# A scan kernel's strip products regrouped: bursts of two slots round the four strips, one bank for the exponents

## What is computed

```python
z, xBC, dt_raw = split(u @ in_proj_w.T)          # z 1024, x 1024, B 128, C 128, dt 64 columns
xBC = silu(conv4(xBC) + conv_b)                  # causal, 4 taps
dt = softplus(dt_raw + dt_bias);  dA = -exp(A_log) * dt
# chunks of 64 tokens, 64 heads of 16 columns; cs = cumsum(dA) in the chunk
Y_diag = sum_s (C_c . B_s) * exp(cs_c - cs_s) * dt_s * x_s     # s <= c, within the chunk
states = sum_s B_s * exp(cs_end - cs_s) * dt_s * x_s           # carried from chunk to chunk
Y_off  = (C_c . state before) * exp(cs_c)
y = Y_diag + Y_off + x * D
yg = y * silu(z);  out = (yg * rsqrt(mean(yg^2) + eps) * norm_w) @ out_proj_w.T
```

## Time and profile before

| | |
|---|---|
| runs | 2022.22, 2024.91, 2026.64 us; median 2024.91 |
| profiled execution | 2034.44 us, its span 2032.5 us |
| busy in the span | PE 1847.0 us (91%), DVE 1419.1 (70%), POOL 983.9 (48%), ACT 921.0 (45%) |
| mean granted TensorE clock | 0.969 of full speed |

### The profile page before, as it was taken

One profiled execution on the slowest core, in us unless ns is written; L12 is line 12 of the kernel. 1 busy time (PEld: TensorE's weight loads), 2 busy tenths in 40 slices (PEclk: granted clock), 3 DMA queues, 4 the chain that ended last, 5 costly groups with the idle time before them and its releaser, 6 DMA issues. The chain is left out here.

```text
span 2032.5 us, 37312 instructions
## 1 busy us (share of the span) xinstructions
PE 1847.0 (91%) x11168; PEld 986.0 (49%) x11168; DVE 1419.1 (70%) x2295; ACT 921.0 (45%) x1647; POOL 983.9 (48%) x1031
## 2 busy tenths in 40 slices
PE   3699999989998998998999899898999999999998
PEld 1255555646545555554654555655334334334333
DVE  6758668666857766875875676875776766765765
ACT  2453354253444334425334434423664654754753
POOL 0045345434525434542542543555764764764754
PEclk9899999999999999999989999889999999999999
DMA  6110140131122014113012201813010110110110
GB/s 200 46 45 25 40 104 26 34 75 39 43 48 80 24 45 101 25 39 86 28 42 55 68 24 50 212 34 71 7 57 32 34 59 26 36 62 26 36 42 31
DMA packets 212566, 109.54 MB, mean 54 GB/s; under 512 B 131642, under 2 KB 183542, under 8 KB 212390
## 3 DMA queue, kind: packets, MB, share of 16 engines
q1 hardware_dynamic: 212390, 107.37, 19.8%
HBM read 80.57 MB, written 26.76 MB: 53 GB/s over the span
## 5 line engine op out<-in xcount | busy, mean ns | idle before, releaser
L1015 ACT ACTIVATE decay<-ps_d 128x512 f32<-128x512 f32 x256 | 151.7, 593 | 383.1 <-PE ps_d L766 381.8
L777 PE MATMUL ps_yd<-mix,xpad 128*32 128x64 f32 x4096 | 281.6, 226 | 31.7 <-DVE y L1326 30.7
L777 PEld LDWEIGHTS ps_yd<-mix,xpad 128*32 128x32 f32 x4096 | 242.6, 113 | 122.6 <-issue 93.2
L1600 POOL TENSOR_TENSOR xend<-xpad,decay 128x256 f32<-128x256 f32 x256 | 180.6, 725 | 228.3 <-PE ps_yo L799 198.2
L708 PE MATMUL ps_in<-u_hi,w_hi 128*128 128x512 f16 (+1 forms) x608 | 238.5, 392 | 52.8 <-DVE u_lo L1188 32.3
L1290 DVE TENSOR_TENSOR mix<-decay,gb 128x512 f32<-128x512 f32 x256 | 222.4, 874 | 54.9 <-ACT gb L1002 31.9
L708 PE MATMUL ps_in<-u_lo,w_hi 128*128 128x512 f16 (+1 forms) x608 | 237.7, 391 | 0.0
L708 PE MATMUL ps_in<-u_hi,w_lo 128*128 128x512 f16 (+1 forms) x608 | 236.9, 390 | 0.0
L730 PE MATMUL ps_in<-w_out,zg 128*128 128x512 f32 x512 | 230.8, 604 | 6.7 <-DVE pre L1201 6.7
L1201 DVE SCALAR_TENSOR_TENSOR pre<-ps_in,cws,pre 128x511 f32<-128x511 f32 (+2 forms) x240 | 178.8, 745 | 14.2 <-ACT pre L954 8.4
L954 ACT ACTIVATE pre<-ps_in,cb,cws 128x512 f32<-128x512 f32 x80 | 62.2, 777 | 231.9 <-PE ps_in L708 231.9
(11 more groups left out here) (194 smaller groups left out, 3877.2 us busy)
## 6 DMA issues: line engine op xcount, KB each, us to landing
ebc<-e_dram SPq DMA_DIRECT2D x256, 64.0 KB, 2.6
u<-u_t SPq DMA_DIRECT2D x9, 1024.0 KB, 5.1
res<-u_tok SPq DMA_DIRECT2D x32, 256.0 KB, 2.7
x_dram<-res SPq DMA_DIRECT2D x32, 256.0 KB, 2.0
xa<-x_dram SPq DMA_DIRECT2D x8, 1024.0 KB, 6.1
xr<-x_dram SPq DMA_DIRECT2D x32, 256.0 KB, 2.7
out<-xr SPq DMA_DIRECT2D x32, 256.0 KB, 2.0
fw_words<-gu_words SPq DMA_DIRECT2D x32, 176.0 KB, 2.7
```

The source lines that it names most:

```text
L777: last = mm(ps_yd[g * 32:(g + 1) * 32, k * CH:(k + 1) * CH], xpad[:, c % 2, k * NG + g, :], mix[:, g, k, :], start=True, stop=True, tile_p ...
L1015: ac(decay[:, n % NG, :, :].rearrange("p a b -> p (a b)"), ps_d[n % 2][:, :], ACT.Exp).then_inc(e_done, 1)
L1600: g_.tensor_tensor(xend[:, g:NP:NG, :], xpad[:, c % 2, g:NP:NG, :], decay[:, g, :, CH - 1:CH].broadcast_to([P, CT, 2 * HD]), ALU.mult).the ...
```

## The change

- **Strips.** The groups of heads are cut anew: group g now holds 8 neighbouring pairs of heads (g x 8 to g x 8 + 7) instead of every fourth. The 8 products of a group then go to the strips 0, 1, 2, 3, 0, 1, 2, 3 (`strip = e % NG`) instead of all to strip g.
- **Bursts.** TensorE does `within` of two slots together, at the second of them (g = 1 and g = 3), after the slot's projection.
- **Banks.** ps_yd becomes two banks, one for even and one for odd chunks; ps_d becomes one. The strip products of chunk c wait for y_all of chunk c - 2, and the exponent product of slot n for the exponential of slot n - 1. The feed-forward phase takes the same eight banks in another order.
- **Order.** y_all goes from VectorE's slot g = 0 to g = 1, behind mixing; gate from g = 1 to 2, square from 2 to 3, sum_squares from g = 3 to g = 0 of the chunk after; q0, q1, q2 to slots 13, 21, 29.
- **DMAs.** ld_dram and the constant rows are laid out by the new groups: 18 stores of the parts for a batch instead of 6, 17 loads of constants instead of 9. load_head is called at SyncE's slot 28 instead of 30.

The diff, cut to its core:

```diff
-BODY_USES = [..., (11, "x0"), (12, "q0"), (14, "o0"), ..., (20, "q1"), (22, "o1"), ..., (28, "q2"), (30, "o2")]
+BODY_USES = [..., (11, "x0"), (13, "q0"), (14, "o0"), ..., (21, "q1"), (22, "o1"), ..., (29, "q2"), (30, "o2")]
-        ps_d = [bank("ps_d0"), bank("ps_d1")]
-        ps_t, ps_s, ps_yd, ps_yo = bank("ps_t"), bank("ps_s"), bank("ps_yd"), bank("ps_yo")
+        ps_d = bank("ps_d")
+        ps_yd = [bank("ps_yd0"), bank("ps_yd1")]
+        ps_t, ps_s, ps_yo = bank("ps_t"), bank("ps_s"), bank("ps_yo")
...
-        ps_gu = [ps_yd] + ps_d + ps_in + [ps_t, ps_s, ps_yo]
+        ps_gu = [ps_yd[1], ps_d, ps_yd[0]] + ps_in + [ps_t, ps_s, ps_yo]
...
                     for h2 in range(2):
-                        sp.dma_start(ld_dram[b, :, :, h2, t].rearrange("r q t -> q r t"),
-                                     ld_parts[row + h2 * NP:row + (h2 + 1) * NP, :, :]).then_inc(parts_out, 16)
+                        for j in range(NG):
+                            heads = slice(row + h2 * NP + j * CT, row + h2 * NP + (j + 1) * CT)
+                            sp.dma_start(ld_dram[b, :, :, j, h2, t].rearrange("r e t -> e r t"), ld_parts[heads, :, :])\
+                              .then_inc(parts_out, 16)
...
-                    if n == 30 and st.proj is not None:
+                    if n == 28 and st.proj is not None:
                         load_head(b + 1)
...
             def exponents(b, n):
-                need(pe, e_done, b * SLOTS + n - 1)
-                mm(ps_d[n % 2][:, :].rearrange("p (k t) -> p k t", k=CT), lhs_d[0:94, c % 2, g, :],
-                   rhs_d[0:94, c % 2, g:NP:NG, :], start=True, stop=True).then_inc(d_full, 1)
+                need(pe, e_done, b * SLOTS + n)
+                mm(ps_d[:, :].rearrange("p (k t) -> p k t", k=CT), lhs_d[0:94, c % 2, g, :],
+                   rhs_d[0:94, c % 2, g * CT:(g + 1) * CT, :], start=True, stop=True).then_inc(d_full, 1)
...
             def within(b, n):
                 if g == 0:
                     pe.wait_ge(t_free, (b * NC + c) * NA + 3)
-                    need(pe, y_done, b * NC + c)
-                for k in range(CT):
-                    last = mm(ps_yd[g * 32:(g + 1) * 32, k * CH:(k + 1) * CH], xpad[:, c % 2, k * NG + g, :],
-                              mix[:, g, k, :], start=True, stop=True, tile_position=(0, g * 32))
+                    need(pe, y_done, b * NC + c - 1)
+                for e in range(CT):
+                    tile, strip = 2 * g + e // NG, e % NG
+                    last = mm(ps_yd[c % 2][strip * 32:(strip + 1) * 32, tile * CH:(tile + 1) * CH],
+                              xpad[:, c % 2, g * CT + e, :], mix[:, g, e, :], start=True, stop=True,
+                              tile_position=(0, strip * 32))
...
                     use_in(st, n)
-                    within(b, n)
+                    if g % 2 == 1:
+                        within(b, n - 1)
+                        within(b, n)
                     if g == 1 and c > 0:
                         from_before(b, c)
...
-                    if g == 0 and c > 0:          # VectorE
-                        y_all(b, c - 1)
                     if n + 2 < SLOTS:
                         mixing(b, n + 2)
                     if g == 0 and c > 0:
                         add_state(b, c - 1, 0)
                         add_state(b, c - 1, 1)
+                    if g == 1 and c > 0:
+                        y_all(b, c - 1)
...
-                    if g == 1 and c > 0:          # GpSimd
+                    if g == 2 and c > 0:
                         gate(st, c - 1)
...
-                    if g == 3 and c > 0:
-                        sum_squares(b, c - 1)
+                    if g == 0 and c > 1:
+                        sum_squares(b, c - 2)
...
+                sum_squares(b, NC - 2)
                 gate(st, NC - 1)
                 sum_squares(b, NC - 1)
```

37 lines of the change are left out of this document (21 added, 16 removed).

## The result

The changed kernel takes 2062.21 us (median of 2058.13 to 2064.95) against 2023.76 for the kernel before beside it: a ratio of 1.017, with a 95% interval of 1.014 to 1.020. It is slower by 1.7% (by the two medians alone 1.9%, 38 us), where 1945 us had been forecast, a gain of 4%. The span of its profiled execution is 2063.1 us, and the mean granted TensorE clock falls from 0.969 to 0.912. The profiled execution of the kernel before (2034.4 us) lies 10 us above its median and this one 3 us, so spans show only 31 of the 38 us.

What follows compares the result with a forecast made beforehand. TensorE was taken as the busiest engine, with VectorE limiting next. Six inner batches at 10.7 us (64) plus 8 each for first and last gave 80 us: 2034.4 to 1954.4, less 9.5 for the profiled run, 1945; range 1915 to 1992.

Steps and rivals of the forecast that it cites:

- Step 1: TensorE's ps_yd products: strips overlap at 0.028 us a matmul, so a double burst costs 1.10 us instead of 2.20.
- rival (b): ps_yd products: four strips don't run together, a matmul stays at 0.056 us; 1990 us, chance 12%.
- (c): Rival on the ps_yd products: strips reach 0.014 us a matmul, but VectorE binds B and C; 1934 us, chance 6%.
- Step 2: Single exponent bank: TensorE waits about 0.3 us in six even slots a batch and 2.1 us at e1, partly hidden.
- A to C: Inner-batch windows: A from rows' landing to o0, B to o1, C to o2; forecast about 33.5, 34 and 30.6 us.
- Step 3: Second ps_yd bank, moved y, gate and squares: the 3.9 us wait for y goes; the other moves cost nothing.
- Step 4: More DMA stores and loads: 6 us more issue on SyncE, covered; cost nothing, 1 us at most.
- What is late next: Inner batch after the change: gains of 4.2, 4.5 and 2.3 us in A, B, C and 0.7 elsewhere, together 11.7.
- Less 1 us for a clock that drops after the new waits: TensorE clock term in each inner batch, after new waits of 2 to 3.5 us for VectorE: 11.7 becomes 10.7 us.
- rival (a): VectorE binds earlier as its operations stretch beside GpSimd's work: 5 to 7 us a batch, 1970 to 1985 us, chance 19%.
- the exponent bank at 2079: Rival for slower: single exponent bank ties TensorE to ScalarE's queue, 0.6 us a slot over 224 slots; chance 6%.
- 0.92 for faster: Forecast's chance that the whole kernel gets faster, against 0.02 for same and 0.06 for slower.

Runs made afterwards that it cites:

- e4: Kernel before with products going round the four strips and bursts of two slots, all else as it was: 2006.5 us, 0.9895.
- e1: Changed kernel with sum_squares moved ahead of the to_end steps on GpSimd in slots g = 0: 2025.03 us, 0.9987.
- e12: e6 with one exponent bank instead of two: 1989.57 us, 0.9798.
- e5: e1 with 26 useless matmuls ahead of TensorE's wait for the state in three slots of each batch with projections: 1981.61 us, 0.978.
- e6: e4 with 12 useless matmuls ahead of the bursts of three slots in each batch with projections: 1971.13 us, 0.9726.
- e8: e5 with one more VectorE reduction (1.745 us) ahead of the additions to the state, 24 in all: 2033.01 us, 1.0023.
- e11: Kernel before with bursts of two slots alone, strips in their old order: 2011.27 us, 0.992.
- e10: Kernel before with useless matmuls alone, 16 ahead of the rows' wait at slot 5 and 12 ahead of slot 20's burst: 2010.06 us, 0.9892.
- e7: e1 with all products of a slot in one strip again, bursts, banks and order kept: 2007.36 us, 0.9898.
- e3: Kernel before with products going round the four strips alone, single bursts, two exponent banks, y in its old place: 2025.01 us, 0.9987.

## Why the prediction was wrong, step by step

**The account.** By ratios: before 1.000; round and bursts on it 0.9895 (e4); the single exponent bank, the second ps_yd bank and y's new place 0.9987 (e1), 19 us, of which the bank makes about 15 if it costs here what it costs in e12; the place of `sum_squares` on GpSimd 1.017, 37 us more. And across all of these, filling the waits is worth 42 us (e5) and 34 (e6).

**Step 1, the products: right in kind, mis-sized in pace.** The term was 32 x 0.028 + 0.20 = 1.10 us. The next matmul follows a double burst after 0.59 us:

```profile
657.25 0.65 PE L784 MATMUL ps_yd<-mix,xpad 128*32 128x64 f32 x32
657.84 2.00 PE L794 MATMUL ps_yo<-bc,state 128*128 128x64 f32 x16
```

With 0.09 at the entry 0.68; the saving is 1.52 a pair, the outer bound of the range. Four strips do run together. In a window of 0.11 us of that line, as in the earlier trace rows, 23 matmuls are under way instead of 6 or 10, and (0.22 + 0.11) / 23 is 14 ns from start to start in the mean:

```profile
657.50:657.61 0.11, 0.11 (x23) 0.11 (x16) 1.00 0.42 126
```

The error was to take the rate of two strips as that of four, 0.028 and 0.033, although the reason behind it (one strip takes a matmul each 0.056) gives 0.014 for four. The Trainium skill, "TensorE: Matmul & The Clock Gate", Wait — 56ns, not 53.3ns?, gives a floor of about 25 ns from start to start; with 14 ns it doesn't hold here for products in different column strips. The Trainium skill, the same page, Part 3, says that weight loads overlap matmuls in flight only where the row group differs; all strips here use all rows, and in this window 16 weight loads are under way beside the 23 matmuls, so that doesn't hold either. By mechanism rival (b) is out and (c) is in, but (c)'s time, 1934, isn't.

**Step 2, the single exponent bank: right.** 2 us at e1 of each tail were forecast and 1.99 came:

```profile
611.07 0.39 PE L772 MATMUL ps_d<-rhs_d,lhs_d 94*128 94x512 bf16 x1 [1.99 <-ACT decay L1026]
```

In A to C 2 us a batch were forecast, 16 in all; e12 gives 8.5. The cover by the rows' DMA was partly there, as said. Nothing of the miss lies here. (In the sum for C the forecast adds the 0.3 us of this wait where they should be taken off; it changes nothing, as VectorE was taken to bind C.)

**Step 3, the moved steps: this failed.** The sentence was "gate, squares and the q products follow one slot on; GpSimd is busy half of A to C at the most, ScalarE less, and the output projections want the gated chunks one chunk later: nothing." The reading was off (GpSimd is busy 22.21 of 38.53 us in B, 58%), but the error was to look at its load and not at what stands ahead in its queue. `sum_squares` was to come from slot g = 3 to g = 0 of the chunk after, where `to_end` waits for TensorE's new state of that slot, and q stands behind this on TensorE's own queue. The page's groups of the kernel before had a row that tells it, which I had not taken up:

```profile
L1600 POOL TENSOR_TENSOR xend<-xpad,decay 128x256 f32<-128x256 f32 x256 | 180.6, 725 | 228.3 <-PE ps_yo L799 198.2
```

Nearly all of this step's idle time, 198 us, ends with TensorE's new state; whoever is put behind it in the same slot inherits the wait. The price is 37 us (e1). The text asked itself for the case of the batch's end alone (`sum_squares(6)` ahead of `gate(7)`), and missed the ordinary slots.

**Step 4, the DMAs: right.** No wait at e0 for the head's rows appears, and in batch 3 none for the rows in slot 5 either, 3.9 us before; e12 shows the same trade, a later slot 0 against a shorter wait for the rows.

**What is late next, and the clock: this failed, and by more.** "Less 1 us for a clock that drops after the new waits" was a term of 1 us in each inner batch; the lost clock of the scan grew by 118 us, 15 a batch, and e5 shows that 42 us of time hang on it even with GpSimd's order mended. The new waits were priced with little more than their own length. In fact a wait of 3 us for VectorE is followed by up to 10 us at half rate (the window from 668.75), in which stands the work that VectorE then waits for; the wait is paid again in the clock. The row that should have told it was in the text: A at a clock of 0.93, behind a wait of 3.9 us for the rows.

**VectorE as the next limit: rival (a) is what is left.** With the clock held and GpSimd's order mended (e5) A, B and C are 36.0, 34.5 and 32.9 us, 103.4 together. Against 109.1 before that is 5.7 us a batch (6.9 in the mean of all eight), in (a)'s "5 to 7 us a batch", where the forecast had 11.0. The time, 1981.6, is in its 1970 to 1985 too, but partly by luck: e5 is not the changed kernel, and it still loses 22 us more of clock than the kernel before. The reason given for (a) holds only in part: mixing takes 0.97 us in the mean in the changed kernel but 0.89 in e1 and e5, where the sums of squares stand elsewhere, and 0.87 before. What binds is less the length of VectorE's operations than that its dense stretch and TensorE's (state, transposes, output projection, 9.4 us) take turns, which e8 shows by its price: 1.745 us more make A 2.0, B 2.2 and C 2.5 us longer. B came out as forecast (34.5 for 34), A and C are 2.5 and 2.3 us over; in C VectorE is busy 30.6 us, where the forecast had counted on its 27.0 of before, so work of other stretches has come into it.

**The rivals for slower.** The forecast named one, the exponent bank at 2079. Slower came, but from a queue order that no rival named. 0.92 for faster was too sure: a part of the change that is costed at nothing by a busy share alone, with three queues involved, deserves a rival of its own.

**Open.** The fall of the clock was prevented by useless work, not by useful work; whether a useful order of TensorE's queue (a projection in the gap) would do as well wasn't tried. Of the 19 us between e4 and e1, 4 are not told apart from noise. The second ps_yd bank and y's new place were not run by themselves, nor was the round over the strips on a kernel with bursts and filled waits (e11 with fills).

## What to carry to other kernels

When two engines take turns, work saved on the busier one can turn into waits, and here each wait of 3 us was followed by up to 10 us at half the TensorE clock, in exactly the work that the other engine waits for: cost a wait with what runs behind it, and try a few useless matmuls in the gap before judging a change (they gave 42, 34 and, in the kernel before, 22 us). A step that moves a slot on an idle engine isn't free: read what stands ahead of it in that engine's queue and whom this waits for, and who waits for the moved step, and not how busy the engine is. Of a group of parts, build each one alone, and with the waits filled: without the fills strips and bursts together showed 21 us (e4), with them 34 (e6 against e10).

## What the runs showed of the hardware

- fp32 products of 64 columns into four column strips by turns start 14 ns apart in the mean (the changed kernel, 32 in 0.65 us, drain included), four times as fast as the 56 ns within one strip (the kernel before, 16 in 1.08). Weight loads of other strips don't hold them up: 16 of them are under way in the same window of 0.11 us as 23 matmuls.
- Without turns, bursts of different strips run together at their border: 32 matmuls, 16 in each of two strips, take 1.72 us to the next one (e11), not the 2.02 of two single bursts.
- This kernel got faster by added work on its busiest engine (e5, 42 us; e6, 34; e10, 22), and by slower products (e7, 18 us).
- The granted clock was 0.50 for 10.2 us at or behind waits of TensorE of 2.8 to 3.7 us (the changed kernel from 668.75, 706.3 and 743.8; e3 from 653.6, 691.2 and 728.7), and 1.00 where the last wait was filled (e5, B of batch 3).
- The same 16 matmuls of an output projection take 6.87 us to the next instruction with the clock held (e5, 641.73 to 648.60), and 7.70 (677.30 to 685.00) behind a wait in the changed kernel; before it was 7.04.
